# A mixture-of-experts layer: normalising each row inside the expert loop instead of in rounds after it

## The reference

```python
probs = softmax(flat @ gate_W)                       # 8 experts
topk_w, topk_idx = top_k(probs, 2)                   # two experts for each row
out = 0.5 * gelu(flat @ shared_W + shared_b)
for e in range(8):
    h = gelu(flat @ W1[e] + b1[e])                   # 256 -> 1024
    out = out + combine[:, e:e+1] * (h @ W2[e] + b2[e])   # 1024 -> 256
out = layernorm(out) * gamma + beta
x = x + out
```

## Time and profile before

| | |
|---|---|
| time, median of 3 runs | 792.94 us |
| the three runs | 788.49, 792.95, 792.94 us |
| the profiled execution | 788.47 us |
| its span in the trace | 786.6 us |
| mean granted TensorE clock | 0.971 |
| TensorE matmuls | 714.2 us busy, 91% |
| VectorE | 304.1 us busy, 39% |
| ScalarE | 443.9 us busy, 56% |
| GpSimd | 147.2 us busy, 19% |

### The profile page before, as it was taken

One profiled execution on the slowest core, in us unless ns is written; L12 is line 12 of the kernel. 1 busy time (PEld: TensorE's weight loads), 2 busy tenths in 40 slices (PEclk: granted clock), 3 DMA queues, 4 the chain that ended last, 5 costly groups with the idle time before them and its releaser, 6 DMA issues. The chain is left out here.

```text
span 786.6 us, 19149 instructions
## 1 busy us (share of the span) xinstructions
PE 714.2 (91%) x7240; PEld 476.2 (61%) x7241; DVE 304.1 (39%) x1010; ACT 443.9 (56%) x759; POOL 147.2 (19%) x140
## 2 busy tenths in 40 slices
PE   4978999999999999998998989999999999999720
PEld 2435445454544444444454566999999999999710
DVE  5772311201152544549666472145312211221136
ACT  2746989988898988965745541332333233233213
POOL 2020050100000000020012343144222212212414
PEclk9997999999999999999999999999999999999875
DMA  9576948982113030307435346767767677777444
GB/s 206 145 231 190 295 122 280 294 258 65 35 50 103 3 104 15 90 22 238 144 118 162 112 159 232 246 175 212 212 176 208 208 193 205 193 207 205 78 120 107
DMA packets 83858, 126.23 MB, mean 160 GB/s; under 512 B 11090, under 2 KB 69740, under 8 KB 81450
## 3 DMA queue, kind: packets, MB, share of 16 engines
q1 hardware_dynamic: 76248, 114.26, 47.1%
q0 software_dynamic: 7536, 10.95, 7.9%
HBM read 82.85 MB, written 42.33 MB: 159 GB/s over the span
## 5 line engine op out<-in xcount | busy, mean ns | idle before, releaser
L844 ACT ACTIVATE arena<-ps 128x1024 f32<-128x1024 f32 x256 | 240.9, 1034 | 32.9 <-PE ps L1858 32.8
L1858 PE MATMUL ps<-arena 99*32 99x512 bf16 x2048 | 161.9, 388 | 2.8 <-issue 2.4
L1835 PE MATMUL ps<-arena 128*32 128x256 f32 x2048 | 158.5, 380 | 0.0
L2188 PE MATMUL ps<-arena 128*128 128x128 f32 x1120 | 133.6, 279 | 4.9 <-issue 4.0
L2188 PEld LDWEIGHTS ps<-arena 128*128 128x128 f32 x1120 | 132.9, 195 | 7.4 <-issue 4.3
L2200 PE MATMUL ps<-arena,xh_tag 128*128 x560 | 126.8, 379 | 1.2 <-DVE arena L1584 1.2
L2200 PEld LDWEIGHTS ps<-arena,xh_tag 128*128 128x128 f32 x560 | 103.7, 190 | 14.2 <-issue 1.6
L955 ACT COPY arena<-ps 128x256 f32<-128x256 f32 x35 | 13.0, 372 | 163.2 <-PE ps L2175 163.2
L748 POOL DMA_INDIRECT sums_by_row<-arena x39 | 60.2, 1544 | 204.2 <-DVE arena L1584 203.0
L1835 PEld LDWEIGHTS ps<-arena 128*32 128x32 f32 x2048 | 65.1, 111 | 51.9 <-issue 1.9
L966 ACT ACTIVATE xh_tag<-ps,arena 128x128 f32<-128x128 f32 x280 | 76.5, 392 | 10.3 <-PE ps L2188 10.3
(11 more groups left out here) (249 smaller groups left out, 771.0 us busy)
## 6 DMA issues: line engine op xcount, KB each, us to landing
arena<-in_L_ffn_W SPq DMA_DIRECT2D x43, 1024.0 KB, 6.9
rows_by_expert<-arena SPq DMA_DIRECT2D x9, 1950.0 KB, 14.8
arena<-q_parts SPq DMA_DIRECT2D x90, 128.0 KB, 2.6
arena<-k_parts SPq DMA_DIRECT2D x42, 128.0 KB
q_parts<-arena SPq DMA_DIRECT2D x12, 384.0 KB, 2.5
arena<-rows_by_expert SPq DMA_DIRECT2D x35, 130.0 KB, 3.1
arena<-in_L_ffn_b SPq DMA_DIRECT2D x35, 128.0 KB, 3.1
k_parts<-arena SPq DMA_DIRECT2D x8, 384.0 KB, 2.5
```

The costliest lines, as they stand in the source:

```text
L844: nc.scalar.activation(probs_of(stage, h), ps[:, 2 * (u % 2):2 * (u % 2) + 2, :].rearrange("p a n -> p (a n)"), ACT.Exp, scale=float(D) ** ...
L1835: last = nc.tensor.matmul(ps[32 * h:32 * h + 32, 4 + half, at:at + 256], v_grp[n % 2][:, kt, h, :], probs_of(stage, h)[:, 256 * part:256 * ...
L1858: last = nc.tensor.matmul(ps[c:c + 32, 2 * (u % 2) + half, :], k_stk[buf][:, h, P * st + c:P * st + c + 32], q_stk[buf][:, h, 512 * half:5 ...
L2188: last = nc.tensor.matmul(ps[:, 4 * buf + half, P * c:P * (c + 1)], w1_buf[:, buf, k, at:at + P], xs_t[:, buf, k, :], start=(k == 0), stop ...
```

## The change

Four things are changed together.

1. **No sums in DRAM, no rounds at the end.** `row_parts` holds three parts of each row side by side: the result of the row's lower expert, the shared part, and `x` (now with the last bias). When a tile's result is there, the rows for which this tile's expert is the lower one are scattered to `row_parts`, the other rows are ignored by an index out of range (`SKIPPED` is added to it). One tile later, VectorE adds up the rows for which this was the higher expert, normalises them (`normalised`), and GpSimd scatters them to the output. The gain is multiplied by -0.125 beforehand, to fit the Newton steps that replace the square root.
2. **The rounds that may be left out come first.** If k of them are left out, every engine but GpSimd jumps to a start at tile 2k and raises its semaphores to the counts it would have had (`begin`, `start_*`). Tile numbers are shifted to match. GpSimd goes through all 39 tiles.
3. **The bias column** is copied by ScalarE instead of VectorE.
4. **Layer 2** writes alternately to PSUM banks 6 and 2 and waits for `y_sum` of two tiles earlier instead of `y_ready` of one.

Rows carry two more floats. `row_parts`' first part is set to zero during attention (2 MB, 0.9 MB before). The additions of the last bias to `x_sb` move from the loop to GpSimd ahead of the scatters of chunks 0 to 2, and to VectorE for chunk 3.

The diff, cut to its core:

```diff
@@ begin: replaces may_run
+        def begin(eng, flags, start):
+            def from_round(k):
+                if k == MAYBE:
+                    start(k)
+                    return
+                with eng.If_ne(flags[MAYBE - 1 - k], 0):
+                    start(k)
+                with eng.If_eq(flags[MAYBE - 1 - k], 0):
+                    from_round(k + 1)
+            from_round(0)
@@ SP
+            for ch in range(3):
+                sp.wait_ge(x_final, ch + 1)
+                store_part(ch, 2, x_sb, x_out)
             for ch in range(2):
                 store_base(ch)
...
+            def start_sp(k):
...
+                for j in range(2):
+                    load_w1(expert(2 * k + j), j)
+                sp.wait_ge(scattered, 16 * 2 * NT)
+                for j in range(2):
+                    load_rows(slots_of(2 * k + j), j)
+                    load_b2(expert(2 * k + j), j)
+                sp.wait_ge(x_last, 1)
+                store_part(3, 2, x_sb, x_out)
+                for ch in (2, 3):
+                    store_base(ch)
+                sp.wait_ge(xs_ps, 2 * k + 1)
+                sp.wait_ge(tag_ready, 2 * k + 1)
+                load_rows(slots_of(2 * k + 2), 0)
+                sp.wait_ge(h_ps, 4 * k + 2)
+                load_w1(expert(2 * k + 2), 0)
+                for i in range(k, MAYBE):
+                    round_sp(i)
+            begin(sp, run_flags(nc.sync), start_sp)
+            with sp.Fori(MAYBE, PAIRS) as i:
                 round_sp(i)
@@ GpSimd
-                nc.gpsimd.indirect_dma_start(
-                    out=sums_dram, out_offset=bass.IndirectOffsetOnAxis(ap=rows, axis=0),
-                    in_=y_sb[:, buf, :], in_offset=None, compute_op=ALU.add).then_inc(landed, 16)
+            def read_parts(s):
+                pool.wait_ge(tag_ready, s + 1)
+                if s >= 1:
+                    pool.wait_ge(y_landed, 16 * s)
+                if s >= 2:
+                    pool.wait_ge(out_ready, s - 1)
+                nc.gpsimd.indirect_dma_start(out=parts_in[:, s % 2, :], out_offset=None, in_=parts_dram, in_offset=rows_at(last_row_at, s),
+                                             bounds_check=NT * P - 1, oob_is_err=False).then_inc(parts_landed[s % 2], 16)
+            def write_first(s):
+                pool.wait_ge(y_ready, s + 1)
+                nc.gpsimd.indirect_dma_start(out=part_rows, out_offset=rows_at(first_row, s), in_=y_sb[:, s % 2, :], in_offset=None,
+                                             bounds_check=3 * NT * P - 1, oob_is_err=False).then_inc(y_landed, 16)
+            def write_out(s):
+                pool.wait_ge(out_ready, s + 1)
+                nc.gpsimd.indirect_dma_start(out=out_rows, out_offset=rows_at(last_row_at, s), in_=out_sb[:, s % 2, :], in_offset=None,
+                                             bounds_check=NT * P - 1, oob_is_err=False).then_inc(out_landed[s % 2], 16)
+            read_parts(0)
+            for s in range(FINAL):
+                write_first(s)
+                read_parts(s + 1)
+                if s >= 1:
+                    write_out(s - 1)
+            for s in (FINAL - 1, FINAL):
+                write_out(s)
@@ VectorE
+            def result(buf, s, landed):
...
+                if not (isinstance(s, int) and s < 2):
+                    dve.wait_ge(y_landed, 16 * s - 16)
...
+            def normalised(buf, s, landed):
...
+                dve.wait_ge(parts_landed[buf], landed)
+                dve.wait_ge(y_ready, s + 1)
+                linked(nc.vector.tensor_tensor(z_sb, parts_in[:, buf, 0:D], parts_in[:, buf, D:2 * D], ALU.add))
+                linked(nc.vector.tensor_tensor(z_sb, z_sb, y_sb[:, buf, :], ALU.add))
+                nc.vector.memset(ln_t, 0.0)
+                linked(nc.vector.bn_stats(ln_stats, z_sb))
+                nc.vector.memset(ln_t, 0.0)
+                linked(nc.vector.bn_aggr(ln_mv, ln_stats))
+                linked(nc.vector.tensor_scalar(ln_v[0], ln_mv[:, 1:2], 4e-5, None, ALU.add))
+                nc.vector.tensor_scalar(ln_v[1], ln_v[0], 0.25, None, ALU.mult)
+                nc.vector.tensor_scalar(ln_v[2], ln_v[0], 0.0625, None, ALU.mult)
+                linked(nc.vector.tensor_scalar(ln_t.bitcast(I32), ln_v[0].bitcast(I32), 1, None, ALU.logical_shift_right))
+                linked(nc.vector.tensor_scalar(ln_r.bitcast(I32), ln_t.bitcast(I32), -1.0, float(0x5F3759DF), ALU.mult, ALU.add))
+                for v in ln_v:
+                    linked(nc.vector.tensor_scalar(ln_t, ln_r, ln_r, v, ALU.mult, ALU.mult))
+                    linked(nc.vector.scalar_tensor_tensor(out=ln_r, in0=ln_t, scalar=-3.0, in1=ln_r, op0=ALU.add, op1=ALU.mult))
...
+                linked(nc.vector.scalar_tensor_tensor(out=out_sb[:, buf, :], in0=z_sb, scalar=ln_mv[:, 0:1], in1=ffn_g_sb,
+                                                      op0=ALU.subtract, op1=ALU.mult))
+                nc.vector.scalar_tensor_tensor(out=out_sb[:, buf, :], in0=out_sb[:, buf, :], scalar=ln_r, in1=parts_in[:, buf, 2 * D:3 * D],
+                                               op0=ALU.mult, op1=ALU.add).then_inc(out_ready, 1)
+            def round_dve(i):
                 for o in range(2):
+                    s = 2 * i + (o + 1)
+                    tags(o, 2 * i + (o + 2))
+                    result(1 - o, s, 16 * i + 16 * (o + 1))
+                    normalised(o, 2 * i + o, 16 * i + 16)
...
+            tags(0, FINAL)
+            result(1, FINAL - 1, 16 * (PAIRS + 1))
+            normalised(0, FINAL - 2, 16 * (PAIRS + 1))
+            result(0, FINAL, 16 * (PAIRS + 2))
+            for s in (FINAL - 1, FINAL):
+                normalised(s % 2, s, 16 * (s // 2 + 1))
@@ TensorE
-                    pe.wait_ge(y_ready, taken)
+                    pe.wait_ge(y_sum, taken)
...
-                    last = nc.tensor.matmul(ps[:, 6, 0:D], hid_t[:, buf, k, :], w2_sb[:, bass.ds(e, 1), k, :].squeeze(1),
+                    last = nc.tensor.matmul(ps[:, Y_BANK[buf], 0:D], hid_t[:, buf, k, :], w2_sb[:, bass.ds(e, 1), k, :].squeeze(1),
```

More of the change, by code:

```diff
@@ L735, in _ @@
             for ch in range(NT // CHUNK):
+                if ch < 3:
+                    pool.wait_ge(xh_ready, NT + CP + CHUNK * (ch + 1))
+                    for t in range(CHUNK * ch, CHUNK * (ch + 1), 2):
+                        last = nc.gpsimd.tensor_tensor(x_sb[:, t:t + 2, :], x_sb[:, t:t + 2, :],
+                                                       ffn_b_sb.unsqueeze(1).to_broadcast([P, 2, D]), ALU.add)
+                    last.then_inc(x_final, 1)
+                else:
+                    pool.wait_ge(u_ps, 2 * 4)
+                    for rows in (first_row, last_row_at):
+                        last = nc.gpsimd.iota(rows, [[0, SLOT_TILES]], base=int(SKIPPED), channel_multiplier=0)
+                    last.then_inc(indices_set, 1)
+                    pool.wait_ge(indices_set, 1)
+                if ch == 0:
+                    pool.wait_ge(rows_set, 4)
                 pool.wait_ge(slot_ready, ch + 1)
@@ L752, in _ @@
-            for n in range(1, 2 * SURE + 2):
-                if n >= 2:
-                    pool.wait_ge(sums_set, 16 * (n - 1))
-                add_result((n - 1) % 2, n, row_used[:, (n - 1) % 2:(n - 1) % 2 + 1], sums_set)
-                if n <= NT // 2:
-                    rows = x_sb[:, 2 * n - 2:2 * n, :]
-                    last = nc.gpsimd.tensor_tensor(rows, rows, ffn_b_sb.unsqueeze(1).to_broadcast([P, 2, D]), ALU.add)
-                if n == NT // 2:
-                    last.then_inc(x_shifted, 1)
@@ L761, in _ @@
[L761 to L772 removed]
+            pool.wait_ge(parts_zero, 16)
@@ L1441, in choose @@
                 nc.vector.tensor_tensor(both, pick1, pick2, ALU.add).then_inc(chosen, 1)
+                link(nc.vector.tensor_tensor(last_rank, rank1, best, ALU.min))
             def place(ch):
@@ L1545, in _ @@
             link(nc.vector.tensor_scalar(expert_rank, expert_rank, float(EXPERTS), None, ALU.add))
-            for i in range(SURE, PAIRS):
-                last = nc.vector.tensor_scalar(run_f[:, i - SURE:i - SURE + 1], ends[:, EXPERTS - 1:EXPERTS], 2.0 * i + 3, None, ALU.is_gt)
-            link(last)
-            nc.vector.tensor_copy(run, run_f)
-            link(nc.vector.tensor_reduce(last_f, run_f, AX.X, ALU.add))
-            nc.vector.tensor_scalar(last_tile, last_f, 2.0, 2.0 * SURE + 2, ALU.mult, ALU.add)
@@ L1659, in _ @@
[L1659 to L1670 removed]
+            for t in range(NT - CHUNK, NT, 2):
+                last = nc.vector.tensor_tensor(x_sb[:, t:t + 2, :], x_sb[:, t:t + 2, :], ffn_b_sb.unsqueeze(1).to_broadcast([P, 2, D]), ALU.add)
@@ new lines, in _, with tags @@
+            last.then_inc(x_last, 1)
+            nc.vector.memset(skipped, SKIPPED)
+            nc.vector.memset(parts_in, 0.0)
+            nc.vector.memset(out_sb, 0.0)
+            link(nc.vector.memset(y_sb, 0.0))
+            def tags(buf, s):
```

(14 more changed lines are left out.)

414 lines of the change are left out of this document (173 added, 241 removed).

## The result

The changed kernel takes 798.56 us (median of 11 runs, 794.18 to 810.83), the one before 792.94 (11 runs, 788.49 to 795.44): 1.0071 times as long, 95% interval 1.0045 to 1.0097. Forecast was 784. The profiled execution after took 796.88 us, its span 795.0.

A forecast was written before the change was run, and what follows sets the result against it. TensorE was taken to bound the loop without a gap, but to idle near the end. The terms -8.2 - 15.3 + 9.5 + 5.0 = -9.0 us, carried to the median of 792.94, gave 784 us; range 770 to 802.

The forecast's parts named there:

- Step 3: Ahead of the loop: skipped tiles still pass through GpSimd, now first, and delay the loop's early tiles, +9.5 us.
- is hidden under these 8: Ahead of the loop: later starts from flags, jumps and weights add nothing to the empty tiles' 8 us.
- Step 5: Ahead of the loop: the additions to x_sb moved to GpSimd, the extra zeroing and related small costs, counted at nothing.
- Step 1: Before the last tile: the skipped rounds leave the end, so TensorE's gap before the last layer 1 goes, -8.2 us.
- Step 2: Behind the last layer 2: normalisation rounds and stores go, leaving 18.0 us against 33.3, -15.3 us.
- Step 4: Expert loop: normalised ahead of the loads on VectorE makes weights 0.5 us late, 0.16 us per tile, +5.0 us.
- E: Rival: other tiles run, or the stretch ahead of the loop suffers; about 790 to 800 us, chance 0.05.
- A: Rival: front and loop absorb it, empty tiles cost 2 us and weights land in 5.3; 771 us, chance 0.15.
- B: Rival: in the loop the weights are late by the full 1.5 us, loop 15.5; 794 us, no change, chance 0.20.
- C: Rival: VectorE becomes the loop's bound at 7.93 us per tile; slower by 11, 804 us, chance 0.10.
- D: Rival: GpSimd is the bound, range-checked issues taking 1.54 us, 7.6 per tile; slower by 8, 801 us, chance 0.08.
- The sign: Whole kernel: forecast faster by 9.0 us; chances 0.48 faster by over 1%, 0.33 within 1%, 0.19 slower.

The follow-up runs named there:

- e1: The changed kernel with no flags loaded and no jumps at the start, the start for two rounds left out written straight: 802.07 us.
- e3: The changed kernel without GpSimd's additions of the last bias ahead of the scatters: 795.41 us.
- e5: The changed kernel without flags, jumps and GpSimd's four empty tiles, the additions ahead of the scatters kept: 786.41 us.
- e4: The changed kernel without flags, jumps, GpSimd's four empty tiles and the additions ahead of the scatters: 779.78 us.
- e12: e7 with TensorE loading its flags ahead of its last two shared results, the cases in their old order: 784.24 us.
- e9: e7 with the case of most rounds left out asked first and TensorE's flags loaded early: 780.00 us.
- e7: The changed kernel with empty transfers issued at once, the additions on VectorE behind the last index, SyncE's first loads and stores ahead of its jump: 784.30 us.
- e2: The changed kernel with GpSimd issuing nothing for the four empty tiles, waits lowered to fit: 790.40 us.
- e10: The kernel before the change with 77 inert indirect transfers added during the attention: 790.40 us.
- e11: The kernel before the change with 65 inert indirect transfers added during the attention: 785.31 us, a single run.

## Why the prediction was wrong

**Step 3, the front: +9.5 forecast, +33.4 measured (9.0 ahead of the index, 24.4 behind it). This is the step that failed,** in three places.
- *"landed at some 498.8"*, the base and x stores. The first read came at 512.18, 13.4 later. 9.0 of it is the later index. Of the other 4.4 only 0.8 are the jumps (in e1 the read follows the index by 26.5 us, here by 27.3); 1.8 are the six stores, which took 5.4 us to issue instead of six times 0.6; the rest isn't told apart.
- *"so an empty tile is 2.5 + 1.27 + 1.27 = 5.0 us"*. The four took 27.4 us where the working had 17.6. The landing was mis-sized at 2.5 us: from the issue of each empty write to the read that waits for it, it was 5.2, 5.4, 2.9 and 5.8 us, so neither the 2.5 of the rows nor the 2.0 worked out beside it holds. In the loop too the writes of L805 and the reads of L799 landed in 3.6 and 5.1 us (medians of all). Why they take longer than the scatters' 2.6 isn't shown. The mechanism behind it, 11.8 us from the first real read to the sixth tile's transposes, was right: 12.1.
- *"is hidden under these 8"*, any later start of the loop. The two add up, since the later index also moves the stores on which the chain of empty tiles waits. What was mostly hidden is the jumps: 2.4 us to the seventh tile with the empty tiles in place, 5.4 without. Flags and jumps on SyncE, "some 3 us", were 9.3. The lower clock, priced 1.5, took 2.7 by the second tile (the first layer 1 is 6.15 us against 3.84) and 2.4 behind the sixth.

**Step 5, "at nothing": the additions on GpSimd.** The working saw in the earlier trace rows that such an addition holds VectorE, and counted "a few such holds as nothing". One hold in the cross-attention set TensorE still for 2.2 us. Leaving the additions out is worth 3.2 us (e3) or 6.6 (e5 to e4) in the medians, and 4.4 in the average date of the index. The Trainium skill (GPSIMD Engine Reference, section 1, Specifications) says that the two engines share their interfaces to SBUF and contend where VectorE's instruction has two SBUF inputs. The trace agrees on both sides. L1411 has two, and the one beside the additions took 3.74 us against 0.69 (the 2.2 of e3's expectation is the mean of it and its undisturbed neighbour); L1406, which reads one of its two from PSUM, kept its 0.69 beside an addition (timeline, kernel after):
```profile
386.19 2.49 POOL L766 TENSOR_TENSOR x_sb<-x_sb,rows_sb 128x512 f32<-128x512 f32 x2 [43.73 <-DVE xh_tag L1470]
386.61 0.69 DVE L1406 TENSOR_TENSOR arena<-ps,arena 128x512 f32<-128x512 f32 x1 [0.56 <-ACT arena L953]
388.33 0.69 DVE L1406 TENSOR_TENSOR arena<-ps,arena 128x512 f32<-128x512 f32 x1 [1.02 <-ACT arena L953]
```
VectorE's busy share, on which the prediction leaned, was also misread: 39% is the mean of the span, in the kernel before it is 21% in the loop and 63% from 380 to 475 us (59.8 of 95). And no such share says whether the next wait is on that engine.

**Step 1, the gap, -8.2: right.** No gap is left on TensorE before the last layer 1. **Step 2, the end, -15.3: nearly right,** 16.5 us behind the last layer 2 instead of 18.0. The order is as worked out: the last `result` at 780.49 behind a `normalised`, two more of 4.8 us each (4.6 forecast), the second waiting 0.48 us for its parts. What was over-counted is the tail: from the last store's issue 2.9 us to the end. In the kernel before, 2.3 of the 33.3 us were GpSimd's drain (777.6 + 8.7 = 786.3, SyncE through at 784.0), which the working took for landing and end of program.

**Step 4, the loop, +5.0: not there.** The working found that nothing was left between W1's issue and its use, with 6.7 us for the landing. It was so, and it held (timeline, kernel after):
```profile
681.22 0.38 SPq L635 DMA_DIRECT2D arena<-in_L_ffn_W  x1
...
688.12 3.73 PE L2232 MATMUL ps<-arena 128*128 128x128 f32 x32
```
6.9 us from issue to layer 1, without a wait. The term mis-sized is the landing of 7.2: there was more traffic beside the weights (229 GB/s against 205), but the DMA's busy share was lower, 0.70 against 0.75, and every tile kept its 7.24 us.

Of the rivals, E (1 in 20) named the place, the stretch ahead of the loop, and the size; it had no price for the empty tiles in it. A was right of the loop and wrong of the front. B, C and D didn't happen: an issue with a range check took 1.0 us, not 1.54, and `normalised` 4.8. The sign was on the wrong side. That the time lies inside the range of 770 to 802 is luck: its upper end was drawn for C, which didn't happen.

## What to carry to other kernels

Moving idle work (skipped rounds, empty transfers) from the end to the start puts it where a chain forms behind it: count it one behind the other, with the waits that join it to what comes before, and issue what needs no order at once. Put jumps behind the loads that they delay; the likeliest case first shortened TensorE's stand, though its worth in time wasn't clear of the noise. A cost found hidden must be looked at again when its cover goes: the jumps were worth 2.4 us with the chain of empty tiles in place and 5.4 without it, and TensorE's own came forward once its rows were there in time. When executions of one kernel scatter by several us ahead of the change, compare from a fixed point behind the scatter.

## What the runs showed of the hardware

- An engine's jump over a whole start (on TensorE hundreds of instructions) cost several us: TensorE stood 6.8 us with two of them and the flags loaded (e12), at most 2.9 with one, the shortest (e9). SyncE took 9.3 us for three flags and its jumps; its first W1 load followed the index by 11.1 us in the kernel after, 6.0 with the jumps behind the load (e7) and 3.3 with neither flags nor jumps (e1).
- GpSimd's last DRAIN comes in a few lengths, each repeated to 0.01 us in the kernels that have it: 2.91 us in eight kernels of the changed family, 9.78 in the three that issue nothing for the empty tiles (e2, e4, e5), 8.71 before, 5.12 with the inert transfers (e10, e11). Where it is long it ends the span, up to 7.3 us after SyncE has seen the last landing (e2, e4, e5).
- A VectorE instruction with two SBUF inputs took 3.73 to 3.74 us instead of 0.69 beside two additions of GpSimd, in all five kernels that have them there; one that reads PSUM and SBUF kept its 0.69 beside them.
- An empty indirect write, with all indices out of range, is not free: 1.0 us of issue, and another 1.9 to 4.8 us until the read that waits for it.
